# One program for all stages, W_in quantised inside the end of cross-attention, W_out spread over four blocks, and x2 formed by VectorE

## The reference, cut to what matters

```
x1  = layernorm(x  + self_attention(x))          # projections, rope, causal exp-sums, a small MLP
x2  = layernorm(x1 + cross_attention(x1, ctx, bias))   # 16 heads of 32, 154 keys, out @ w_out
out = layernorm(x2 + ffn(x2))

ffn(x):  W_in  (512 x 2048)  rounded to int8 steps, one scale per column (127 / max|.|)
         W_out (2048 x 512)  rounded to int8 steps, one scale per row
         x_q    = round(x * 32767 / max|x|)      # ONE maximum over the whole x2
         hidden = gelu(x_q @ W_in_q + b_in)
         h_q    = round(hidden * 32767 / max|hidden|)   # ONE maximum over all of hidden
         return h_q @ W_out_q + b_out
```

## Time and profile before

| | |
|---|---|
| median of 3 runs | 2305.74 us (2298.34 to 2331.83) |
| the profiled execution | 2303.44 us, its span 2301.7 us |
| PE busy | 2099.1 us, 91% |
| VectorE busy | 1730.8 us, 75% |
| ScalarE busy | 1081.3 us, 47% |
| GpSimd busy | 842.9 us, 37% |
| granted TensorE clock, mean | 0.952 |
| self-attention | until about 575 us |
| cross-attention with its drain | about 575 to 1305 us |
| FF1, its first matmul to its last | 1346.5 to 1817.0 us |
| FF2, its first matmul | 1841.8 us |

### The profile page before, as it was taken

The page is one execution under the profiler, slowest core; times in us unless marked ns, Lnnn a source line. Parts: engine busy times, 40 slices in busy tenths (PEclk is TensorE's granted clock), DMA queues, the critical chain, the costliest instruction groups (busy, mean ns, idle before and its releaser), DMA issues. The chain is left out here.

```text
span 2301.7 us, 32961 instructions
## 1 busy us (share of the span) xinstructions
PE 2099.1 (91%) x11904; PEld 1162.5 (51%) x11904; DVE 1730.8 (75%) x3281; ACT 1081.3 (47%) x1522; POOL 842.9 (37%) x819
## 2 busy tenths in 40 slices
PE   7999999984999999998999468899999599999997
PEld 3444444431777776776777233344444244444443
DVE  6768686865787897997998365966665488888885
ACT  1444444442555554554555133344444465555551
POOL 3122221322154555555555532222222134444442
PEclk9999999996798998998999779999999899999999
DMA  6344342457789889979974278788888457667762
GB/s 231 108 136 143 103 147 100 119 132 186 199 191 216 224 187 209 239 189 208 242 160 113 74 224 276 233 271 269 269 275 272 194 205 230 232 224 230 232 223 81
DMA packets 386947, 448.53 MB, mean 195 GB/s; under 512 B 279463, under 2 KB 279751, under 8 KB 368353
## 3 DMA queue, kind: packets, MB, share of 16 engines
q1 hardware_dynamic: 322736, 286.14, 45.4%
q0 software_dynamic: 64048, 160.28, 22.5%
HBM read 259.00 MB, written 138.73 MB: 173 GB/s over the span
## 5 line engine op out<-in xcount | busy, mean ns | idle before, releaser
L1656 PE MATMUL ps_h<-xT,w 128*128 128x512 f16 x2048 | 453.4, 384 | 22.7 <-ACT h L1487 12.7
L1896 PE MATMUL ps<-w,g_hi 128*128 128x512 f16 x1024 | 389.3, 380 | 28.4 <-DVE g_lo L1834 28.4
L1896 PE MATMUL ps<-w,g_lo 128*128 128x512 f16 x1024 | 389.3, 380 | 0.0
L1656 PEld LDWEIGHTS ps_h<-xT,w 128*128 128x128 f16 x2048 | 201.7, 99 | 268.6 <-issue 18.7
L1487 ACT ACTIVATE h<-ps_h,b_in_sb,col_scale 128x512 f32<-128x512 f32 x256 | 197.7, 777 | 262.8 <-PE ps_h L1656 235.6
L1225 PEld LDWEIGHTS ps_o<-vm,pT 128*128 128x128 f32 x2048 | 293.4, 199 | 13.2
L1059 DVE TENSOR_REDUCE stack<-ps_m 128x2 f16<-128x308 f32 x512 | 243.8, 478 | 59.6 <-PE ps_m L1179 47.6
L1225 PE MATMUL ps_o<-vm,pT 128*128 128x33 f32 x2048 | 279.9, 262 | 0.0
L1017 ACT ACTIVATE pT<-logit 128x512 f32<-128x512 f32 x320 | 198.7, 624 | 113.8 <-DVE logit L1077 112.8
L1749 POOL TENSOR_TENSOR rstd<-vare,minus_half 128x1 f32<-128x1 f32 x64 | 154.2, 2410 | 212.0 <-DVE vare L1852 212.0
L1563 DVE TENSOR_REDUCE amax_t<-h 128x1 f32<-128x2048 f32 x64 | 146.2, 2284 | 102.5 <-ACT h L1487 101.6
(11 more groups left out here) (175 smaller groups left out, 3840.2 us busy)
## 6 DMA issues: line engine op xcount, KB each, us to landing
hidden<-h POOLq DMA_DIRECT2D x64, 1024.0 KB, 6.7
hT<-hidden SPq DMA_DIRECT2D x64, 1024.0 KB, 6.0
xc<-x_cols SPq DMA_DIRECT2D x16, 1024.0 KB, 5.1
xr<-x_rows SPq DMA_DIRECT2D x16, 1024.0 KB, 5.4
x_rows<-x POOLq DMA_DIRECT2D x16, 1024.0 KB, 4.8
x1t<-x_rows SPq DMA_DIRECT2D x64, 256.0 KB, 3.7
bt_main<-bias_main SPq DMA_DIRECT2D x16, 1024.0 KB, 6.6
xres<-x_rows SPq DMA_DIRECT2D x64, 256.0 KB, 4.0
```

What stands on the lines that cost most here:

```text
L1656: mm = pe.matmul(ps_h[f % 4][:], w1[:, c, f * P:(f + 1) * P], xT[:, e, a, :, c, :], start=(a == 0 and c == 0), stop=(a == 1 and c == KC - 1))
L1896: mm = pe.matmul(ps[t][:], g[:, e, f, t * P:(t + 1) * P], w2[:, f, :], start=(f == 0 and a == 0), stop=(f == FC - 1 and a == 1))
```

## The change

1. All four stages are one block; the semaphores and a few small tensors last from cross-attention to the end. The staging buffer of the weights is the buffer that held cross-attention's bias (`bt_main`), and the transposed W_in lies where its bias rows were. The stages' order on each engine is now kept by semaphores alone.
2. `finish` moves from GpSimd to VectorE: k = 2 of the same quarter, on tile q-7. GpSimd keeps the root and the store. The magnitude moves from k = 6 on tile q-8 to k = 4 on tile q-7.
3. W_in is loaded group by group as the bias groups come free, and quantised wholly on VectorE after quarters 62, 63, 65 and 67. All its transposes stand ahead of block 0.
4. The maximum of x2 stays in SBUF. The loads of the first two x2 blocks are issued before the end of the drain.
5. W_out is loaded and quantised at the end of blocks 1, 3, 5 and 7, one group each.

The diff, cut to its core:

```diff
@@ cross-attention, GpSimd
-            def finish(s, b, t):
+            def store(s, b, t):
...
-                pool.wait_ge(rstd_ready, tile + 1)
-                if not (isinstance(tile, int) and tile < 2):
-                    pool.wait_ge(x2_out[e], 16 * (2 * (4 * s + b) + t // 2))
-                    pool.wait_ge(amax_part, tile - 1)
-                pool.tensor_tensor(spacer[:], minus_half[:], minus_half[:], ALU.mult)
-                pool.tensor_scalar(x2t[:, e], y[:, e], mv[:, e, 0:1], rstd[:, e:e + 1],
-                                   ALU.subtract, ALU.mult).then_inc(x2_ready, 1)
                 pool.wait_ge(x2_ready, tile + 1)
...
-                finish(*span_at(s, b, i, -7))
+                store(*span_at(s, b, i, -7))
@@ cross-attention, VectorE
+            def finish(nu, t):
...
+                dve.wait_ge(rstd_ready, tile + 1)
+                if tile >= 2:
+                    dve.wait_ge(x2_out[e], 16 * (2 * nu + t // 2))
+                    dve.wait_ge(amax_part, tile - 1)
+                dve.tensor_scalar(x2t[:, e], y[:, e], mv[:, e, 0:1], rstd[:, e:e + 1],
+                                  ALU.subtract, ALU.mult).then_inc(x2_ready, 1)
...
-                    if k == 6:
-                        magnitude(*at(n, i, -8))
+                    if k == 2:
+                        finish(*at(n, i, -7))
+                    if k == 4:
+                        magnitude(*at(n, i, -7))
@@ FF1, SyncE
+                for q in tail.quarters:
+                    tail.sp(q)
+                    g = q - tail.first - 1
...
+                    if 0 <= g < FG:
+                        sp.wait_ge(tail.biased, 20 * (NBLK - 1) + 5 * (g + 1))
+                        load_w(g)
...
+                    if n in (2, 4, 6, 8):
+                        sp.wait_ge(w_int_ready, n // 2)
+                        load_w(FG + n // 2 - 1)
@@ FF1, VectorE
+                def quantise_w_in(g):
+                    weight_scales(g)
+                    dve.wait_ge(w_scaled, g + 1)
+                    for c in range(4):
+                        dve.tensor_scalar(w_stage[:, g, c, :], w_stage[:, g, c, :], w_scale[:, g, c:c + 1], ROUND,
+                                          ALU.mult, ALU.add).then_inc(w_shifted, 1)
                     dve.wait_ge(w_shifted, 4 * g + 4)
...
+                for q in tail.quarters:
+                    tail.dve(q)
+                    if q - tail.first in (2, 3, 5, 7):
+                        quantise_w_in({2: 0, 3: 1, 5: 2, 7: 3}[q - tail.first])
+                tail.last_maximum(amax_set)
...
-                        if isinstance(n, int) and n == 1:
-                            quantise_w_out(g)
+                        if g == 3 and n in (1, 3, 5, 7):
+                            quantise_w_out(n // 2)
@@ FF1, TensorE
+                for q in tail.quarters:
+                    tail.pe(q)
+                pe.wait_ge(tail.mx_ready, 32 * NBLK)
+                for k in range(FC):
                     transpose_weights(k)
```

More of the change, by code:

```diff
@@ L762, in over_quarters @@
                         quarter(2 * m + e, i, e)
-            for q in range(QUARTERS - 8, QUARTERS + 9):
+            for q in range(QUARTERS - 8, TAIL):
                 quarter(q // 4, q % 4, (q // 4) % 2)
@@ L773, in over_spans @@
                         quarter(s, b, i)
-            for q in range(QUARTERS - 16, QUARTERS + 9):
+            for q in range(QUARTERS - 16, TAIL):
                 quarter(q // 16, q // 4 % 4, q % 4)
@@ L905, in quarter @@
                     load_bias(s, GROUPS - 1)
-            for q in range(-8, QUARTERS + 9):
+            for q in range(-8, TAIL):
                 quarter(q // 16, q // 4 % 4, q % 4)
+            rest["sp"] = lambda q: quarter(q // 16, q // 4 % 4, q % 4)
         @block.gpsimd
@@ L979, in _ @@
             over_spans(pool, quarter)
[L980 to L984, removed]
+            rest["pool"] = lambda q: quarter(q // 16, q // 4 % 4, q % 4)
         @block.scalar
@@ L1048, in _ @@
             over_quarters(act, quarter)
+            rest["act"] = lambda q: quarter(q // 4, q % 4, (q // 4) % 2)
         @block.vector
@@ L1115, in residual @@
                 dve.tensor_scalar(vare[:, s:s + 1], mv[:, s, 1:2], EPS, None, ALU.add).then_inc(vare_ready, 1)
+            def finish(nu, t):
+                if not inside(nu, t):
+                    return
+                tile = 4 * nu + t
+                e = t % 2
+                dve.wait_ge(rstd_ready, tile + 1)
[4 more added lines that the diff above has]
+                                  ALU.subtract, ALU.mult).then_inc(x2_ready, 1)
             dve.wait_ge(consts_in, 16)
@@ L1278, in _, with feed_forward_stage @@
             over_quarters(pe, quarter)
-def feed_forward_stage(nc, x2_rows, amax_x, w_in_rows, b_in, w_out_rows, b_out, identity, hidden, resid, out):
+            rest["pe"] = lambda q: quarter(q // 4, q % 4, (q // 4) % 2)
+    return CrossAttentionTail(quarters=range(TAIL, QUARTERS + 9), first=TAIL, biased=biased, lg_done=lg_done,
+                              mx_ready=mx_ready, amax_part=amax_part, x2_out=x2_out, **rest)
+def feed_forward_stage(nc, x2_rows, w_in_rows, b_in, w_out_rows, b_out, hidden, resid, out, block, sems, shared, tail):
     NBLK = BATCH * SEQ // BLK
@@ L1294, in keep @@
         def keep(name, shape, dt):
-            return outer.enter_context(nc.sbuf_tensor(name, shape, dt))
+            return outer.enter_context(nc.sbuf_tensor(name, shape, dt, side="right"))
         w2 = keep("w2", [P, FC, DIM], F16)
@@ L1729, in load_row @@
                     sp.dma_start(xrb[:, t % 2], src[:, :, t, :].rearrange("n p d -> p (n d)")).then_inc(xrb_in[t % 2], 16)
+                for g in range(FG):
+                    sp.wait_ge(h_out[g], 16 * NBLK)
+                sp.wait_ge(xres_out, 16 * NBLK)
                 for g in range(FG):
@@ L1861, in finish @@
                                       ALU.subtract, ALU.mult).then_inc(out_ready, 1)
+                for g in range(FG):
+                    dve.wait_ge(h_out[g], 16 * NBLK)
                 scale_rows(0, 0)
```

206 lines of the change are left out of this document (93 added, 113 removed).

## The result

| | before | after |
|---|---|---|
| median (runs) | 2307.07 us (4) | 2499.99 us (4) |
| lowest to highest | 2298.34 to 2331.83 | 2496.22 to 2509.57 |
| profiled execution, span | 2303.4, 2301.7 | 2498.53, 2496.7 |
| mean granted clock | 0.952 | 0.914 |

The ratio is 1.0849, with a 95% interval of 1.0811 to 1.0887: 8.5% slower. Forecast were 2607 us and slower; the sign and the range (2380 to 2710) held, the size did not: +195 us of span instead of +304.

A forecast was written before the change was run, and what follows sets the result against it. Cross-attention was taken as bound by TensorE and VectorE, both full, with other limits in other stages. 2303.4 + 330 + 8 + 27 - 29 - 25 - 7 = 2607 us; range 2380 to 2710.

The forecast's parts named there:

- The wait: Cross-attention quarters: VectorE stands 3.0 us for GpSimd's rstd ahead of the x2 tile, TensorE 2.8 us; undisturbed quarter 13.4 us.
- rival 1: Cross-attention: the clock stays up despite the 2.8 us stretches; whole 2387 us; chance 0.19.
- rival 2: Cross-attention: the clock never comes back, 20.9 us per quarter, +507 us; whole 2784 us; chance 0.07.
- rival 3: Cross-attention: rstd is ready before VectorE wants it, tile costs 0.55 against 0.40 us idle; whole 2270 us; chance 0.05.
- The clock: Quarters 7 to 59: three in four stretches let the clock fall, quarters then 18.9 instead of 13.4 us; total +330 us.
- The wait's own part: Quarters 7 to 59: with all 52 at 13.4 us and no clock fall, the loss is +117 us.
- Quarters 59 to the drain: Quarters without maxima, 59 to 63: +5 us for tile and wait, +3 for a low clock, together +8 us.
- The drain: Last quarters, with W_in groups of 5.8 us on VectorE: the 35.4 us grow by +27 us, ends +15 and +35.
- the tile's wait: Drain, quarters 63 to 65: waiting ahead of the x2 tile adds 3 us.
- GpSimd's contention: Drain: W_in groups beside comb_lo might be slowed by shared SBUF interfaces, making the sum some 5 us higher.
- The joins and FF1: Without barriers the join to FF1 gives -29 us and that to FF2 -7; FF1's removed TensorE waits give -25.
- Rival 4: Joins: the barriers were hidden, so the joins give nothing; whole 2643 us; chance counted inside the forecast's 0.66.

The follow-up runs named there:

- experiment 1: The changed kernel with GpSimd computing the root rstd ahead of comb_lo instead of behind it; 2286.7 us, ratio to before 0.9913.
- experiment 3: The kernel before with only x2 moved to VectorE, its maximum at k = 4, separate programs and barriers kept; 2543.1 us, ratio to before 1.1033.
- Experiment 4: The changed kernel with 18 more matmuls on TensorE ahead of each quarter's sixth max pair, output unaffected; 2430.6 us, ratio to before 1.0557.
- experiment 5: The changed kernel with 8 more matmuls on TensorE ahead of each quarter's sixth max pair, output unaffected; 2420.2 us, ratio to before 1.0493.
- experiment 2: The changed kernel with x2 formed on GpSimd again and its maximum back at k = 6, the rest kept; 2294.1 us, ratio to before 0.9958.
- Experiment 8: The kernel of experiment 1 with three W_in groups behind quarters 65, 66, 67 and the fourth behind the last maximum; 2269.8 us, ratio to before 0.9835.
- experiment 6: The kernel before with only the four W_out groups spread over FF1's blocks 1, 3, 5 and 7; 2298.75 us, ratio to before 0.9953.
- experiment 7: The changed kernel with a GpSimd addition of about 0.9 us, read by nobody, ahead of each root; 2544.0 us, ratio to before 1.1031.

## Why the prediction was right, and where it was not

- **The wait.** Right in place, releaser, count and size: 3.0 us forecast, 2.97 seen in a like quarter, and an undisturbed quarter of 13.6 us (13.4 forecast). Experiments 1 and 3 show that it is the cause: with it 783 to 787 us for the 52 quarters, without it 584. Rivals 1 to 3 are out: the clock neither stayed up nor stayed down, and rival 3 falls by the wait itself. But rival 3's claim that the tile is cheap once the root is early was right: experiment 1 is 10.54 us per quarter, 0.18 above before, where it had 0.15.
- **The clock, the step that failed.** The prediction took three stretches in four to let the clock fall, at 5.5 us each (18.9 against 13.4), so 213 of its 330 us. Experiment 4 measures that part at 79 us. Both factors were too high. It took 2.8 us as an independent trial each time, but a fall makes TensorE late and the next stretch shorter (1.93 us), and there the clock stayed up: 23 falls in 52 quarters, not 39. The 1.91 us that it took as the lower mark with a fall did not bear that either: at none of the 25 stretches of 1.9 to 2.4 us did the clock fall. And it added the whole excess of the 16.1 us quarter to the new one, though that quarter had no slack and the new ones have 2.8 us of it: a fall costs 79.6 / 23 = 3.5 us. The low phase of that example was longer too. The engines of the kernel before around it:

```profile
702.00:703.00 1.00, 0.06 (x4) 0.09 (x4) 0.00 (x0) 0.12 (x1) 0.42 (x2) 0.92 1.09 332
704.00:716.00 12.00, 11.40 (x48) 8.49 (x49) 7.21 (x17) 6.17 (x11) 4.42 (x6) 0.50 1.03 165
716.00:717.00 1.00, 1.00 (x10) 0.92 (x9) 0.67 (x2) 0.45 (x1) 0.82 (x1) 0.76 0.86 355
```

  The clock was low there for 13.7 us, from 702.8 to 716.5, against 10.2 here. What was not worked out: 9.7 us of work at half speed put TensorE 4.8 us behind, and the idle stretches of 2.6 us take part of that back. So the size came out within the range because the range reached down to a clock that never falls; the likeliest time was 107 us too high. This term was 134 us too high, the others together some 25 us too low.
- **The wait's own part.** Forecast +117, measured 128.5: the quarter is 13.6 us, a term mis-sized by 0.2 us in 52 places. The prediction struck out the 0.40 us that VectorE waits for the projection; in the quarters of 13.6 us of experiment 5 the residual still waits 0.42 us, and part of that is made up by other short waits of VectorE that are gone.
- **Quarters 59 to the drain.** +11 for +8, in kind: the quarters 59 to 61 took 10.04 to 10.34 us where before had 8.4. The wait is there in full (2.98 us), but swallows other idle time of VectorE that before had. The other 6 us come in the last stretch up to the residual, in which the clock is low (0.51 from 1472 to 1485 us) and the residual waits 3.91 us for TensorE.
- **The drain.** +34.3 for +27. The kinds of cost were right, but the first two groups cost 11 and 8 us in the kernel of experiment 1, where the prediction had 5.8 for each: behind the first VectorE waits 4.7 us for a projection at the low clock. Experiments 1 and 2 (no 3.0 us wait, yet 68.5 and 67.4 us) show that the groups alone make 32 of the 34 us; experiment 3 shows that the move alone would make 11, where the prediction had 3 for the tile's wait. The two are not additive. Experiment 8 shows that their place sets the price: 16.6 us for three groups late and one in the all-reduce. The prediction's point that GpSimd's contention might add 5 us was not put to the test: the sixteen shifts in the kernel after took 480 to 486 ns each, but none of them ran beside a `comb_lo` (the four groups of shifts start at 1489.8, 1509.2, 1530.1 and 1544.9 us, the last three `comb_lo` at 1496.4, 1513.5 and 1522.5). The shift of 5109 ns of before did run beside work of GpSimd, a 4.52 us addition of 128x2048. It is one of the four shifts in the first line, which took 1.68 us together elsewhere:

```profile
1451.09 6.31 DVE L1533 TENSOR_SCALAR w_stage<-w_stage,w_scale 128x512 f32<-128x512 f32 x4
1451.79 4.52 POOL L1436 TENSOR_TENSOR xres<-xb,b_out_sb 128x2048 f32<-128x2048 f32 x1
```

- **The joins and FF1.** -29, -25 and -7 forecast; -29.1, -26.8 and -7.1 measured. Rival 4 is out. In FF1 the sum was right and its split not tested until experiment 6: the groups alone give 9 us, not the 16 that were given to the waits.
- **The first quarters.** +5 not forecast, and within the scatter of the ten traces (experiment 6).

## What to carry to other kernels

Before a small step moves to another engine, follow its input back through the other engines' lists: what decides is whether the value is made behind something that itself waits for this engine's last step, not what the step costs. Where it is, look for the producer's order first: here two swapped lines were worth 213 us. A cost that comes back each period must be computed as a cycle, with the slack that the cost itself creates, and not as a single example times its count. Work that fills a hole belongs where an engine stands for a fixed latency, like the all-reduce, and not where two engines take turns.

## What the runs showed of the hardware

- The same idle stretch does not always have the same effect: in the kernel after the clock fell at 22 of 26 stretches near 2.65 us, in experiment 7 at 3 of 22 of 2.7 us, in experiment 5 at one of 51 under 1.7 us. What was ahead of them differs: in experiment 7 a low phase ended some 5 us ahead of those stretches, in the kernel after the clock had been up for 18 us or more, with one shorter stretch in it. But the four of the 26 at which the clock stayed up had such work ahead of them as well. It is shown that length alone does not decide; why is open.
- Once down, the clock stayed at 1.2 GHz for 10.2 us in the kernel after (TensorE at work for 9.7 of them), 13.7 us from 702.8 us on in before, about 7 us on the mean in experiment 7, and longer at the start of cross-attention. The engines over 55 us of experiment 2's kernel, TensorE without a gap and the clock never up:

```profile
590.00:645.00 55.00, 55.00 (x262) 46.06 (x261) 34.21 (x68) 21.94 (x37) 7.97 (x7) 0.50 0.64 163
```

  Why it comes back after 10.2 us in one place and not in 55 in another is open too.
- Matmuls whose result nobody reads made the kernel 69 to 80 us faster while the wait beside them stayed. They are no substitute for removing the wait, which gave 213 us.
- A VectorE instruction that takes 0.48 us elsewhere took 5.1 us in the one place of before where it ran beside a 4.52 us addition on GpSimd. That the addition is the cause is likely but not shown by any edit.
